# Interleaving transposes of probabilities with projection and score products in a GNN and attention kernel

## The reference

```python
# layer 0: one of four expert matrices for each graph, then batch norm, relu, residual, layer norm
W = expert_w[top1]
out = adj @ (x @ W)
x = layernorm(x + relu(batchnorm_per_expert(out)))
# layer 1: attention, residual, layer norm
q, k, v = split_heads(x @ Wq.T), split_heads(x @ Wk.T), split_heads(x @ Wv.T)
a = einsum('bhnd,bhmd->bhnm', q, k) * 512 ** -0.5 + 2 * adj
p = softmax(a)                       # rows that are all zero are masked
o = einsum('bhnm,bhmd->bhnd', p, v)
x = layernorm(x + o @ Wo.T)
```

## Time and profile before

| | |
|---|---|
| median of 3 runs | 2258.58 us (2255.59 to 2259.07) |
| profiled execution | 2262.85 us, its span 2261.1 us |
| granted TensorE clock, mean | 0.985 |
| PE busy | 95% of the span |
| DVE, ACT busy | 70%, 70% |
| POOL busy | 13% |
| DMA q1 | 60.9% of 16 engines' span |

### The profile page before, as it was taken

One profiled execution on the slowest core, in us unless ns is written; L12 is line 12 of the kernel. 1 busy time (PEld: TensorE's weight loads), 2 busy tenths in 40 slices (PEclk: granted clock), 3 DMA queues, 4 the chain that ended last, 5 costly groups with the idle time before them and its releaser, 6 DMA issues.

```text
span 2261.1 us, 42446 instructions
## 1 busy us (share of the span) xinstructions
PE 2137.0 (95%) x14627; PEld 1688.9 (75%) x14627; DVE 1581.3 (70%) x4012; ACT 1571.9 (70%) x3509; POOL 301.7 (13%) x659
## 2 busy tenths in 40 slices
PE   6999998689999999999999999999999999999996
PEld 5778886567777777777777777777777777777774
DVE  5888886366767676767676767676767686767675
ACT  3544443287777777777777777777777787777785
POOL 0000000010202020202020202020202020202011
PEclk9999999799999999999999999999999999999999
DMA  6443433677777777777777777777777777777771
GB/s 229 162 159 138 151 127 113 122 114 128 138 127 132 131 132 129 137 126 137 128 127 129 133 129 137 128 133 129 132 127 132 130 138 126 134 129 128 126 106 46
DMA packets 149008, 297.18 MB, mean 131 GB/s; under 512 B 14514, under 2 KB 14546, under 8 KB 148690
## 3 DMA queue, kind: packets, MB, share of 16 engines
q1 hardware_dynamic: 137490, 256.97, 60.9%
q0 software_dynamic: 11328, 37.76, 5.9%
HBM read 110.12 MB, written 50.33 MB: 71 GB/s over the span
## 4 chain that ended last, share of the span: by engine, by line
PE 62%; issue 13%; DMA 10%; DVE 8%; ACT 4%; SPq 1%; POOL 0%; DVEq 0%; ACTq 0%; POOLq 0%
PE bank L605 24%; PE bank L651 16%; PE bank L635 9%; PE bank L620 7%; DMA adj_sb<-in_adj_dram 5%; DMA v<-outT_spill 4%; DVE prob L1166 4%; PE bank L525 2%; PE bank L542 2%; ACT prob L872 2%; PE bank L577 1%; ACT probT L770 1%; SPq L376 1%; DVE z L1130 1%; DVE st_ln L1123 1%
## 5 line engine op out<-in xcount | busy, mean ns | idle before, releaser
L1166 DVE CUSTOM_DVE_ANT_0 prob<-bank,adj_sb 128x512 f32<-128x512 f32 x1024 | 657.2, 685 | 152.9 <-PE bank L620 121.7
L872 ACT ACTIVATE prob<-prob,neg_max 128x512 f32<-128x512 f32 x1024 | 731.5, 723 | 11.2 <-DVE neg_max L1175 7.5
L770 ACT ACTIVATE probT<-bank 128x512 f32<-128x512 f32 x832 | 459.8, 593 | 292.6 <-PE bank L651 288.8
L651 PE MATMUL bank<-ident,prob 128*128 128x128 f32 x4096 | 544.8, 276 | 16.0 <-ACT probT L770 14.7
L651 PEld LDWEIGHTS bank<-ident,prob 128*128 128x128 f32 x4096 | 465.2, 141 | 126.0 <-issue 51.2
L620 PE MATMUL bank<-kp,qp 128*128 128x512 f32 x1024 | 352.7, 426 | 52.4 <-DVE row_max L1166 42.9
L1180 DVE COPY probT<-bank 128x512 f32<-128x512 f32 x192 | 131.7, 686 | 261.4 <-PE bank L651 261.4
L635 PE MATMUL bank<-probT,v 128*32 128x256 f32 x4096 | 248.8, 383 | 0.1
L620 PEld LDWEIGHTS bank<-kp,qp 128*128 128x128 f32 x1024 | 177.6, 191 | 91.8 <-DVE row_max L1166 63.0
L872 ACT ACTIVATION_READ_ACCUMULATOR prob<-prob,neg_max 128x1 f32 x1024 | 203.9, 199 | 0.0
L605 PE MATMUL bank<-woT,oT 128*128 128x512 f32 x768 | 203.5, 401 | 0.0
(11 more groups left out here) (112 smaller groups left out, 2088.3 us busy)
## 6 DMA issues: line engine op xcount, KB each, us to landing
kp<-stage_k SPq DMA_DIRECT2D x256, 256.0 KB, 6.9
qp<-stage_q SPq DMA_DIRECT2D x256, 256.0 KB, 8.2
x_raw<-in_x_dram SPq DMA_DIRECT2D x16, 1024.0 KB, 7.5
adj_raw<-in_adj_t_dram SPq DMA_DIRECT2D x16, 1024.0 KB, 9.6
outT_spill<-outT SPq DMA_DIRECT2D x16, 1024.0 KB, 5.2
v<-outT_spill SPq DMA_DIRECT2D x16, 1024.0 KB, 15.4
z<-in_x_dram POOLq DMA_DIRECT2D x64, 256.0 KB, 3.5
adj_sb<-in_adj_dram SPq DMA_DIRECT2D x64, 256.0 KB, 7.9
```

Source lines behind the costliest of these rows:

```text
L651: ins = nc.tensor.transpose(t_bank[j % 2][:, mt * P:(mt + 1) * P], prob[:, s % 2, j, mt * P:(mt + 1) * P], ident[:, :])
L770: return nc.scalar.activation(dst, src, ACT.Copy, scale=scale)
L872: nc.scalar.activation(prob[:, s % 2, j, :], prob[:, s % 2, j, :], ACT.Exp, scale=2.0, bias=neg_max[:, s % 2, j:j + 1], accum_out=row_sum[ ...
L1166: nc.vector.tensor_tensor_reduce(prob[:, s % 2, j, :], s_bank[j][:, :], adj_sb[:, t, :], 1.0, LOWEST, ALU.add, ALU.max, row_max[:, g % 2, ...
```

## The change

ScalarE's code stays as it is. On TensorE:

- The transposes of a head are no longer four in a row. `prob_block` does one, `dense_product` one product of a slot, and in most places they alternate: transpose, product, transpose, product. In even steps the slot's products are four at the top, four between the transposes of head 0 and four between those of head 1; head 2's transposes are alone. In odd steps they are four each with heads 0, 1 and 2, and nothing stands ahead of head 0. In steps 8 and 9 four go with head 2 and eight behind it.
- The scores of heads 0 to 2 are made two steps ahead: one after each of the first three transposes of head 3, at the end of step s for step s+2. Those of head 3 stay one step ahead; in odd steps they come after the transposes of head 0.
- The wait for `t_bank[0]` (copies of the step before) comes at the top of each step, ahead of the four products of even steps, and `spread_recip` goes up with it.
- Each score product waits for its own bank's reader.

On VectorE `bias_and_max` waits for the transposes of its own head of two steps before, and head 0's comes ahead of the copy of head 3.

```diff
             def scores(b, s, heads):
...
-                if heads[0] == 0:
-                    need(pe, s_max, 64 * b + J * s)
-                else:
-                    pe.wait_ge(s_max, 64 * b + J * s + 1)
                 for j in heads:
+                    if j == 3:
+                        pe.wait_ge(s_max, 64 * b + J * s + 1)
+                    else:
+                        need(pe, s_max, 64 * b + (J * s if j == 0 else J * (s - 1) + j + 1))
...
             scores(0, 0, (3,))
+            scores(0, 1, (0, 1, 2))
...
-                    late = s in XT_EARLY
+                    late = s in XT_EARLY and not last
...
+                    def project(first_product, count):
                         if there:
-                            if half == 0:
+                            if first_product == 0:
                                 pe.wait_ge(*reader[s % 2])
+                            for n in range(first_product, first_product + count):
+                                dense_product(kind, b + rel, i, n, dense_bank[s % 2])
+
+                    def transpose_and_project(j, first_product):
+                        for mt in range(NT):
+                            prob_block(b, s, j, mt)
+                            project(first_product + mt, 1)
...
-                    next_scores((0, 1, 2))
...
-                    if not late:
-                        dense_half(0)
+                    even = s % 2 == 0
+                    t_bank_freed(0, b, s)
+                    if group_end:
+                        spread_recip(b if s else b - 1, s // NT - 1 if s else G - 1)
+                    if even and not late:
+                        project(0, 4)
...
-                    if group_end:
-                        t_bank_freed(0, b, s)
-                        spread_recip(b if s else b - 1, s // NT - 1 if s else G - 1)
-                    next_scores((3,))
+                    if even or late:
+                        next_score(3, 1)
...
-                    if not group_end:
-                        t_bank_freed(0, b, s)
-                    prob_transpose(b, s, 0)
+                    if late:
+                        transpose_alone(0)
+                    elif even:
+                        transpose_and_project(0, 4)
+                    else:
+                        transpose_and_project(0, 0)
+                        next_score(3, 1)
                     t_bank_freed(1, b, s)
-                    prob_transpose(b, s, 1)
+                    if late:
+                        transpose_alone(1)
+                    elif even:
+                        transpose_and_project(1, 8)
+                    else:
+                        transpose_and_project(1, 4)
...
-                    if not late:
-                        dense_half(1)
...
                     pe.wait_ge(pT_act, copies_act(b, s, 1))
-                    prob_transpose(b, s, 2)
+                    if late:
+                        transpose_and_project(2, 0)
+                        project(4, 8)
+                    elif even:
+                        transpose_alone(2)
+                    else:
+                        transpose_and_project(2, 8)
                     pe.wait_ge(pT_act, copies_act(b, s, 2))
-                    prob_transpose(b, s, 3)
-                    if late:
-                        dense_half(0)
-                        dense_half(1)
+                    for mt in range(NT):
+                        prob_block(b, s, 3, mt)
+                        if mt < J - 1:
+                            next_score(mt, 2)
...
                 for j in heads:
+                    need(dve, p_ps, 64 * b + J * (s - 2) + j + 1)
                     wait_apart(dve, s_ps, 64 * b + J * s + j + 1)
...
+                    if ahead:
+                        bias_and_max(nb, ns, (0,))
                     if s > 0 and s - 1 not in ACT_COPIES_3:
                         copy_probT(b, s - 1, 3)
...
-                        bias_and_max(nb, ns, (0, 1, 2))
+                        bias_and_max(nb, ns, (1, 2))
```

More of the change, by code:

```diff
@@ L607, in dense, with dense_product @@
                     ins.then_inc(dense_ps[kind], 1)
+            def dense_product(kind, b, i, n, ps):
+                t, (a, c) = n // 3, PARTS[n % 3]
+                if kind == "o" and i == 0 and n % 3 == 0:
+                    pe.wait_ge(oT_lo, NT * b + t + 1)
+                if kind == "v" and n == 0:
+                    pe.wait_ge(xT_lo, NT * b + i + 1)
+                if kind == "k" and i == 0 and n == 0:
+                    pe.wait_ge(xT_lo, NT * b + NT)
+                if kind in "kq":
+                    w, m = wT[kind][a][:, t, i * P:(i + 1) * P], xT[c][:, t, :]
+                elif kind == "v":
+                    w, m = xT[a][:, t, i * P:(i + 1) * P], wT["v"][c][:, t, :]
+                else:
+                    w, m = oT[a][:, t, i * P:(i + 1) * P], wT["o"][c][:, t, :]
+                ins = mm(ps[:, :], w, m, start=(n == 0), stop=(n == 3 * NT - 1))
+                if n == 3 * NT - 1:
+                    ins.then_inc(dense_ps[kind], 1)
             def scores(b, s, heads):
@@ L646, in spread_recip, with prob_block @@
                 ins.then_inc(r_ps, 1)
[L648 to L653, removed]
+            def prob_block(b, s, j, mt):
+                if mt == 0:
+                    pe.wait_ge(exp_done, 64 * b + J * s + j + 1)
+                ins = nc.tensor.transpose(t_bank[j % 2][:, mt * P:(mt + 1) * P],
+                                          prob[:, s % 2, j, mt * P:(mt + 1) * P], ident[:, :])
+                if mt == NT - 1:
+                    ins.then_inc(p_ps, 1)
             def t_bank_freed(n, b, s):
@@ L690, in batch, with next_score, transpose_alone @@
                     group_end = s % NT == 0 and not (first and s == 0)
-                    late = s in XT_EARLY
-                    def next_scores(heads):
-                        if s + 1 < STEPS:
-                            scores(b, s + 1, heads)
+                    late = s in XT_EARLY and not last
+                    def next_score(j, ahead):
+                        if s + ahead < STEPS:
+                            scores(b, s + ahead, (j,))
                         elif not last:
-                            scores(b + 1, 0, heads)
-                    def dense_half(half):
+                            scores(b + 1, s + ahead - STEPS, (j,))
+                    def project(first_product, count):
                         if there:
-                            if half == 0:
+                            if first_product == 0:
                                 pe.wait_ge(*reader[s % 2])
-                            dense(kind, b + rel, i, (2 * half, 2 * half + 1), dense_bank[s % 2])
-                    next_scores((0, 1, 2))
-                    if s in XT_EARLY and not last:
+                            for n in range(first_product, first_product + count):
[4 more added lines that the diff above has]
+                            project(first_product + mt, 1)
+                    def transpose_alone(j):
+                        for mt in range(NT):
+                            prob_block(b, s, j, mt)
+                    if late:
                         pe.wait_ge(*reader[s % 2])
@@ L710, in batch @@
                         reader[s % 2] = (xT_lo, NT * (b + 1) + XT_EARLY[s] + 1)
[L711 to L712 removed]
+                    even = s % 2 == 0
[4 more added lines that the diff above has]
+                        project(0, 4)
                     if last and s == STEPS - 1:
                         dense("o", b, 1, range(NT - 1), last_o_bank[1])
[L715 to L719 removed]
+                    if even or late:
+                        next_score(3, 1)
+                    if s > 0 and even:
                         weigh_v(b, s - 1, par)
```

1 line of the change is left out of this document (removed).

## The result

| | before | after |
|---|---|---|
| median | 2257.09 us (4 runs) | 2433.65 us (2429.06 to 2437.78, 4 runs) |
| profiled execution | 2262.85 us | 2429.06 us |
| its span | 2261.1 us | 2427.3 us |

The changed kernel takes 1.0778 times as long (95% interval 1.0763 to 1.0794). Forecast were 2396 us in a range of 2310 to 2450: the way and the order of size held, the loss of 177 us was larger than the 137 worked out.

A forecast was written before the change was run, and what follows sets the result against it. TensorE's order and waits were taken as the bound. Added waits and pairs of 12.9 us a batch less 3.9 removed gave 9.0, +137 us in all: 2400 us profiled, 2396 median, range 2310 to 2450.

The forecast's parts named there:

- The price of a pair: On TensorE, a transpose plus a product costs 0.34 us alternated or apart; 5 ns lost per pair, +0.8 us a batch.
- the idle loader: Timeline: the second transpose's load started only with the first transpose at 1315.25, though the loader was free since 1315.16.
- read as more: First rival: weight loads hide deeper, a pair costs 0.26 instead of 0.34 us; 2217 us, chance 0.10.
- The handovers: Head 0's transposes in odd steps except 9 wait for ScalarE's copy of head 2 of the step before; 9.4 us a batch.
- Head 3, whose share the forecast counted in these: About 0.2 us of each odd-step wait already falls on head 3, waiting for head 1's copy across four bare transposes.
- behind the relus: Step 2's two relus take 1.4 us of ScalarE ahead of step 3's copies, delaying head 2 there; +0.5 us a batch.
- The tops of even steps: Waits for bank copies entering even steps: 0.9 us each in steps 4 and 6, 0.1 each in four others; +1.8 and +0.4.
- What goes: Old waits that vanish: 2.9 of 3.5 us for VectorE and 1.0 of 1.3 for ScalarE's copies, 3.9 us a batch.
- step 2's loads: Step 2's waits for the late adjacency tile (1.33 us in one batch) and v's relu, claimed covered by steps 0 and 1's stalls.
- step 8 nothing, since twelve products follow head 1: No added wait for the transposes' bank after step 8, as twelve products follow head 1; 0 us.
- batch 15: Last batch: first eight steps lose 6.2 + 1.8 us, earlier scores shorten the last eight by up to 6; +2 us total.
- VectorE's being late: Fourth rival: head 3's copy comes late behind the next bias, 0.6 us each, +2.4 a batch; 2435 us, chance 0.08.

## Why the prediction was right, point by point

**The price of a pair: right.** The step read from the idle loader was that one load is ahead and each instruction costs its stream or the next load, whoever its neighbour is: 0.34 and 5 ns. Measured are 0.345, against 0.339 for the two apart. The Trainium skill's sentence on loads pulled ahead of running matmuls ("TensorE: Matmul & The Clock Gate", Part 2) is true here of one load and no more; read as more, it would have given a faster kernel, which neither the pair's 0.345 us nor the two kernels with and without alternation show. The 0.8 us a batch that I added for pairs can't be seen in the changed kernel, where the waits come to the whole loss; with only the scores alternated, a pair cost 10 to 20 ns, somewhat more than my value.

**The handovers: right in place and releaser.** The waits at the top of the seven odd steps (1, 3, 5, 7, 11, 13, 15) are 1.38, 0.86, 1.35, 1.66, 1.33, 1.38 and 0.86, 8.8 us, against 1.56, 1.04, 1.52, 1.60, 1.09, 1.56 and 1.04. Head 3, whose share the forecast counted in these, adds 0.25 in the even steps 0, 4, 12 and 14 and in most batches in step 2: 10.0 against 9.4. That these waits cost what they last shows in step 15, 0.84 us longer than before with a wait of 0.86. Head 2 of step 3 waits 0.41 behind the relus, where 0.5 was forecast. The kernel with one exponential moved shows the cause by itself: the tops that it could shorten became shorter by 0.69 to 0.72, one exponential. The tops of even steps together are 2.7 against 2.2; of these the two in steps 4 and 6 are 1.03 and 1.02 against 0.9, and four smaller ones 0.16 each against 0.1.

**What goes: right for VectorE, too hopeful for step 2.** The score waits fell to 0.9 us a batch, where I had left 0.6; step 8 kept 0.30. I had step 2's loads covered whole by the stalls before them; 0.57 for the tile and about 0.3 for a copy behind the relu stayed. That this wait takes up what is won ahead of it was the mechanism I named, and the experiments show it from the other side: the tile's wait grew to 1.2 us with the transposes grouped, to 1.7 with the exponential moved and to 1.6 with work ahead of head 0.

**What was missed.** The step "step 8 nothing, since twelve products follow head 1", and with it the late steps, looked at the transposes' bank alone. In step 9 the slot's first products moved ahead to head 2, and both the bank they write and the tile they read hang on VectorE's `xT_low`: 1.41 us a batch, 20 us in all, shown by putting the slot back. So 10.9 us a batch stand against 9.0: 1.4 of it is step 9, 1.0 the copies' waits (13.4 against some 12.4), 0.3 the scores', less the pairs' 0.8. Outside the middle batches batch 0 lost 10.6 us (9 forecast) and batch 15 7.7 (2 forecast; the chain through VectorE and ScalarE, which the earlier scores were to shorten by up to 6, gave back less than that, and why is not shown). Layer 0, which is the same code, took 4 us less in the profiled execution of the changed kernel than in that of before. Most of these errors have one sign, so it was not their cancelling that kept the time in the range; it lies 16 us below the upper bound.

**The range** held. VectorE's being late, which I had as the way to a larger loss, gave 2435 us, which is where the time came out, but that is chance: its mechanism has a small place in it. VectorE is hardly late for head 3's copy: `weigh_v` waited 5.1 us for it in the 14 batches, 26 times 0.2; the late VectorE that costs is that for `xT` in step 9.

```profile
PE bank L654 <- DVE probT L1224: 5.1, 26, 0.2
```

## What to carry to other kernels

Before two streams of instructions are woven together, read from the loads of the trace whether a pair gets cheaper at all; then list for each buffer what lay between its last write and its next, since weaving moves last writes later and first uses earlier, and for each instruction that moves forward when its inputs are made. A chain on an engine that is busy for two thirds of the time can set the pace over a stretch, and then the order on that engine is what to change. Waits for transfers take up what is won ahead of them, so the transfers come first: moving one load in its queue and the relus that wait for another by one step gave 1.3%, where the reordering of the matrix engine cost 7.8%. And the sum of the waits that an edit takes away is more than its gain where the next wait stands close behind: four of the edits here gave between 45% and 74% of it.

## What the runs showed of the hardware that was not expected

In a stream of pairs the load of the transpose that follows a product starts 0.13 us after the product's own load (1551.53 and 1551.66, with the transpose at 1551.87), where in a stream of one kind it is 0.11; the pair makes up for most of it in the second half, 0.21 instead of 0.23. A head 0 transpose that had waited had its load 0.05 us after ScalarE's copy ended (1549.81 and 1549.86), and at all 98 handovers of the middle batches it is 0.050 to 0.052 us.
